# Gated heads: the head's choice of output expert is applied in the turned layout, by masks made with 0/1 products

## The reference, cut to what matters

```python
q, k = heads(x @ w_q), heads(x @ w_k)              # 8 heads of 64
gates = sigmoid(x @ w_gate)                        # 8 experts for each head and token
sel = argmax(gates, axis=-1)
gm = one_hot(sel, 8) * gates                       # one gate value at one of 8 places
values = einsum('bhne,ehdk,bnd->bhnk', gm, value_experts, x)
attn = softmax(where(causal, (q * 64**-0.5) @ k.T, -big))
out = attn @ values                                # z, 64 wide for each head
out = einsum('bhne,ehkd,bhnk->bhnd', gm, output_experts, out)
x = x + out.sum(over heads)
```

## Time and profile before

| what | value |
|---|---|
| median of three runs | 3925.12 us (3923.46 to 3925.54) |
| the profiled execution: its time, its span | 3947.5 us, 3945.8 us |
| busy, share of the span | PE 3584.7 us (91%), PEld 2967.5 (75%), DVE 2856.1 (72%), ACT 2172.8 (55%), POOL 299.6 (8%) |
| mean granted TensorE clock | 0.968 |
| the stage `gated_heads` | from 2759 us to the end |

### The profile page before, as it was taken

How to read it: one execution, slowest core, us unless ns; L and a number is a source line. 1 busy time by engine, 2 the same in 40 slices (tenths; PEclk the granted TensorE clock), 3 DMA queues, 4 the chain that set the end, 5 groups by cost and what they waited for, 6 DMA issues and landing times. The chain is left out here.

```text
span 3945.8 us, 93353 instructions
## 1 busy us (share of the span) xinstructions
PE 3584.7 (91%) x28930; PEld 2967.5 (75%) x28930; DVE 2856.1 (72%) x9189; ACT 2172.8 (55%) x6677; POOL 299.6 (8%) x382
## 2 busy tenths in 40 slices
PE   6999999899999998079877889998899999999998
PEld 5888888688888886069755656665688888888887
DVE  5666666677777777556567878887877787777786
ACT  5777777677777776235444557776433333333333
POOL 0000000000000000521287000000000000000000
PEclk9999999899999999589989999999999999999999
DMA  2000000100000002422211000000200000000000
GB/s 98 0 0 0 0 0 0 38 33 11 11 11 11 11 11 97 143 92 77 73 43 37 0 20 21 21 21 19 92 12 13 8 11 13 8 13 11 11 11 9
DMA packets 56112, 109.74 MB, mean 28 GB/s; under 512 B 8368, under 2 KB 27184, under 8 KB 55728
## 3 DMA queue, kind: packets, MB, share of 16 engines
q1 hardware_dynamic: 46656, 80.72, 6.5%
q0 software_dynamic: 8464, 26.22, 2.0%
q10 hardware_dynamic: 864, 1.19, 0.1%
HBM read 72.46 MB, written 35.65 MB: 27 GB/s over the span
## 5 line engine op out<-in xcount | busy, mean ns | idle before, releaser
L639 ACT ACTIVATE c_pr<-c_sm,c_nmx 128x256 f32<-128x256 f32 x512 | 254.5, 499 | 153.5 <-DVE c_nmx L485 153.5
L127 PE MATMUL f_ps_out<-f_out_rounded,f_zgT 128*128 128x256 f32 x1024 | 310.3, 303 | 0.0
L128 PE MATMUL f_ps_out<-f_out_rest,f_zgT 128*128 128x256 f32 x1024 | 288.5, 282 | 0.0
L129 PE MATMUL f_ps_out<-f_out_rounded,f_zgT 128*128 128x256 f32 x1024 | 286.3, 280 | 0.0
L639 ACT ACTIVATE a_pr<-a_sm,a_nmx 128x128 f32<-128x128 f32 (+1 forms) x512 | 227.1, 444 | 105.9 <-DVE a_nmx L485 105.8
L485 DVE CUSTOM_DVE_ANT_0 a_sm<-a_ps_s,causal 128x128 f32<-128x128 f32 (+1 forms) x512 | 152.6, 354 | 164.3 <-PE a_ps_s L371 164.3
L2170 DVE TENSOR_TENSOR f_gv<-f_ps_v,f_gm_step 128x512 f32<-128x512 f32 x256 | 175.8, 687 | 124.9 <-PE f_ps_v L129 112.7
L2329 ACT CAST f_zgT<-f_ps_g 128x512 fp32r<-128x512 f32 x256 | 151.4, 591 | 204.8 <-PE f_ps_g L2059 204.8
L1770 ACT ACTIVATE c_pr<-c_ps_s,c_nmx 128x256 f32<-128x256 f32 x512 | 214.2, 500 | 87.5 <-DVE c_nmx L1602 87.5
L485 DVE CUSTOM_DVE_ANT_0 c_sm<-c_ps_s,c_mask 128x256 f32<-128x256 f32 x512 | 186.8, 421 | 92.0 <-PE c_ps_s L371 90.2
L2229 DVE TENSOR_TENSOR f_zgT<-f_ps_g,f_zgT 128x512 fp32r<-128x512 f32 x256 | 176.6, 690 | 77.3 <-ACT f_zgT L2329 73.6
(11 more groups left out here) (380 smaller groups left out, 11382.7 us busy)
## 6 DMA issues: line engine op xcount, KB each, us to landing
f_slot_rows<-f_run POOLq DMA_DIRECT2D x1, 9216.0 KB, 34.7
f_rows<-f_slot_rows SPq DMA_DIRECT2D x72, 128.0 KB, 2.0
f_slot_out<-f_y SPq DMA_DIRECT2D x72, 128.0 KB, 1.9
c_ctx_stage<-in_ctxT SPq DMA_DIRECT2D x32, 256.0 KB, 2.8
small<-in_f_w SPq DMA_DIRECT2D x16, 512.0 KB
x_sb<-in_x SPq DMA_DIRECT2D x8, 512.0 KB, 8.1
small<-in_c_w SPq DMA_DIRECT2D x8, 512.0 KB, 3.8
c_mask_stage<-in_mask SPq DMA_DIRECT2D x16, 256.0 KB, 3.0
```

The source lines that it names most:

```text
L127: nc.tensor.matmul(out, sh, mh, start=start, stop=False, **kw)
L128: nc.tensor.matmul(out, sh, ml, start=False, stop=False, **kw)
L129: return nc.tensor.matmul(out, sl, mh, start=False, stop=stop, **kw)
L639: last = nc.scalar.activation(pr[:, r, i, 0:n], sm[:, j, i, 0:n], ACT.Exp, bias=nmx[:, j, i:i + 1], scale=-1.0, accum_out=sums[:, r, i:i + 1])
```

## The change

Mask and gate value are separated. The gate value (`top`) multiplies the softmax's division in `norm`, as a second pointer, so z comes out of `values` already gated once. The choice itself, now exactly 0 or 1 (`one`), is turned once a batch (`turn_one` on PE into `ps_t`, `take_one` on ACT, four copies of 32 partitions to `oneT`). For each step `spread_one` makes, by products with a constant 0/1 matrix `spread` (built by POOL at the stage's start, behind which PE, DVE and ACT wait by the semaphore `made`), the mask of one expert over 128 rows (two heads of 64) and 256 tokens, two experts for each k, in `ps_g`. z is split into rounded part and rest once a step (`take_zT` on ACT, `rest_z` on DVE), and `gate_z` multiplies both parts by the mask from `ps_g`, two DVE instructions of 128 x 512 for each k, to `zgT`. `back`, `take_z`, `turn_zg`, `take_zgT`, `rest_zgT`, `cut_piece` and `keep_piece` are gone. k now counts pairs of experts, not (j, i); `output` keeps its 12 products for each k, and the output experts lie in another order (`f1_out`). The output's lag is 4 (`OUT_LAG`), while `LAST` stays 5. `choose` takes the minimum of 1 + exp(-logit) and the reciprocal of the 16 minima only, where it took the reciprocal of all 128 values.

```diff
+            nc.gpsimd.memset(one[:], 0.0).then_inc(made, 1)
+            nc.gpsimd.memset(sel, 0.0).then_inc(made, 1)
+            pool.wait_ge(made, 2)
+            nc.gpsimd.affine_select(out=sel, in_=sel, compare_op=ALU.not_equal, fill=1.0, base=0,
+                                    pattern=[[-1, E], [-E, 2], [0, 64]], channel_multiplier=1).then_inc(made, 1)
+            for s in range(STEPS):
+                nc.gpsimd.tensor_copy(oneT[:, s, :], one[:].rearrange("p i s n -> p (i s n)")).then_inc(made, 1)
+            pool.wait_ge(made, 3)
+            nc.gpsimd.tensor_copy(spread[:], sel).then_inc(made, 1)
...
+                if s == STEPS - 2 and j == 0:
+                    pe.wait_ge(oneT_ready, b + 1)
...
-            def back(g, s):
-                pe.wait_ge(zT_ready, g + 1)
+            def turn_one(b):
+                pe.wait_ge(pick_s, PICKS * (b + 1))
+                pe.wait_ge(prT_ready, 2 * (STEPS * b + 2))
                 for i in range(ST):
-                    last = nc.tensor.transpose(ps_z[:, S + i * P:S + (i + 1) * P], zT[:, s % 2, i * P:(i + 1) * P], c.ident[:])
-                last.then_inc(backed, 1)
-            def turn_zg(g, s, k, batches):
-                pe.wait_ge(zg_ready, K * g + k + 1)
+                    last = nc.tensor.transpose(ps_t[:, i * P:(i + 1) * P], one[:, i].rearrange("p s n -> p (s n)"), c.ident[:])
+                last.then_inc(one_ps, 1)
+            def spread_one(g, s, k, b, batches):
                 if late(g, 1) or k:
                     pe.wait_ge(zgT_ready, K * g + k)
-                if s == STEPS - LAST % STEPS and k == 0:
+                if s == 0 and k == 0:
+                    pe.wait_ge(oneT_ready, b + 1)
                     pe.wait_ge(gate_exp, batches)
-                for p in range(E // 2):
-                    last = nc.tensor.transpose(ps_g[:, p * P:(p + 1) * P],
-                                               zg[:, k % 2, 2 * p:2 * p + 2, :].rearrange("p e k -> p (e k)"), c.ident[:])
-                last.then_inc(zg_ps, 1)
+                for n in range(2):
+                    last = nc.tensor.matmul(ps_g[:, n * S:(n + 1) * S], spread[:, 2 * k + n].rearrange("p j m -> p (j m)"),
+                                            oneT[:, s, :], start=True, stop=True)
+                last.then_inc(spread_ps, 1)
 
             def output(g, s, k, b):
-                j, i = k // 2, k % 2
                 pe.wait_ge(zgT_ready, K * g + k + 1)
                 if s == 0 and k == 0 and late(g, STEPS):
                     pe.wait_ge(added, b)
-                if not late(b, 1) and i == 0:
-                    pe.wait_ge(pieces.split, HEADS + 2 * s + j + 1)
-                for p in range(E // 2):
-                    last = product3(nc, ps_out[:, i * D:(i + 1) * D], [t[:, k % 2, p, :] for t in zgT],
-                                    [t[:, 2 * s + j, p, :] for t in w_out], s == 0 and k == 0 and p == 0,
-                                    s == STEPS - 1 and j == 1 and p == E // 2 - 1, skip_group_check=True)
+                if not late(b, 1) and k % 2 == 0:
+                    pe.wait_ge(pieces.split, HEADS + 2 * s + k // 2 + 1)
+                for n in range(2):
+                    for i in range(ST):
+                        last = product3(nc, ps_out[:, i * D:(i + 1) * D], [zgT[:, k % 2, r, n, i * P:(i + 1) * P] for r in range(2)],
+                                        [t[:, 2 * s + k // 2, (2 * k + n) % 4, :] for t in w_out],
+                                        s == 0 and k == 0 and n == 0 and i == 0,
+                                        s == STEPS - 1 and k == K - 1 and n == 1, skip_group_check=True)
...
+                if late(b, 1):
+                    dve.wait_ge(top_kept, STEPS * b)
+                done(nc.vector.tensor_reduce(top[:], gate[:], X, ALU.min))
+                done(nc.vector.tensor_tensor(eq[:], gate[:], wide(top), ALU.is_equal))
                 done(nc.vector.tensor_tensor(eq[:], eq[:], rev[:], ALU.mult))
                 done(nc.vector.tensor_reduce(best[:], eq[:], X, ALU.max))
-                done(nc.vector.tensor_tensor(eq[:], eq[:], wide(best), ALU.is_equal))
                 if late(b, 1):
 
-                    dve.wait_ge(piece, STEPS * b)
-                done(nc.vector.tensor_tensor(gm[:], eq[:], gate[:], ALU.mult))
-            def cut_piece(g, s):
+                    dve.wait_ge(v_gated, K * STEPS * b)
+                done(nc.vector.tensor_tensor(gm[:], eq[:], wide(best), ALU.is_equal))
+                done(nc.vector.reciprocal(top[:], top[:]))
+                if late(b, 1):
+                    dve.wait_ge(one_ps, b)
+                for i in range(ST):
+                    done(nc.vector.tensor_copy(one[:, i, :, 0:2 * E], gm[:, i * HEADS:(i + 1) * HEADS, :].rearrange(
+                        "p (s j) e -> p s (j e)", j=2)))
+                done(nc.vector.tensor_tensor(gm[:], gm[:], wide(top), ALU.mult))
...
-                    last = nc.vector.tensor_scalar(pr[:, r, keys(i)], pr[:, r, keys(i)], inv[:, r, i:i + 1], None, ALU.mult)
+                    last = nc.vector.tensor_scalar(pr[:, r, keys(i)], pr[:, r, keys(i)], inv[:, r, i:i + 1],
+                                                   top_step[:, s, j, i:i + 1], ALU.mult, ALU.mult)
...
+            def rest_z(g, s):
+                dve.wait_ge(zT_round, g + 1)
+                nc.vector.tensor_tensor(zT[:, s % 2, 1, :], ps_z[:, 0:S], zT[:, s % 2, 0, :].bitcast(F32),
+                                        ALU.subtract).then_inc(zT_ready, 1)
...
+                dve.wait_ge(spread_ps, K * g + k + 1)
+                dve.wait_ge(zT_ready, g + 1)
                 if late(g, 1) or k >= 2:
 
-                    dve.wait_ge(zg_ps, K * g + k - 1)
-                nc.vector.tensor_tensor(zg[:, k % 2], z[:, i, 64 * j:64 * j + 64].unsqueeze(1).broadcast_to([P, E, 64]),
-                                        gm_late[:, s, i, j, :].unsqueeze(2).broadcast_to([P, E, 64]), ALU.mult).then_inc(zg_ready, 1)
+                    dve.wait_ge(out_ps, K * g + k - 1)
+                for r in range(2):
+                    last = nc.vector.tensor_tensor(zgT[:, k % 2, r], zT[:, s % 2, r, :].bitcast(F32).unsqueeze(1).broadcast_to([P, 2, S]),
+                                                   ps_g[:].rearrange("p (n s) -> p n s", n=2), ALU.mult)
+                last.then_inc(zgT_ready, 1)
...
             def take_zT(g, s):
                 act.wait_ge(z_done, g + 1)
                 if late(g, 2):
-                    act.wait_ge(backed, g - 1)
-                nc.scalar.copy(zT[:, s % 2, :], ps_z[:, 0:S]).then_inc(zT_ready, 1)
-            def take_zgT(g, k):
-                act.wait_ge(zg_ps, K * g + k + 1)
-                if late(g, 1) or k >= 2:
-                    act.wait_ge(out_ps, K * g + k - 1)
-                nc.scalar.copy(zgT[0][:, k % 2].rearrange("p e s -> p (e s)"), ps_g[:]).then_inc(zgT_round, 1)
+                    act.wait_ge(zgT_ready, K * (g - 1))
+                nc.scalar.copy(zT[:, s % 2, 0, :], ps_z[:, 0:S]).then_inc(zT_round, 1)
+            def take_one(b):
+                act.wait_ge(one_ps, b + 1)
+                for s in range(STEPS):
+                    last = nc.scalar.copy(oneT[0:32, s, :], ps_t[32 * s:32 * s + 32, 0:S])
+                last.then_inc(oneT_ready, 1)
...
-        "f1_out": v["L1_ffn_output_experts"].reshape(4, 2, 8, 64, D).transpose(1, 3, 2, 0, 4).reshape(P, 8, 4, D),
+        "f1_out": v["L1_ffn_output_experts"].reshape(8, 4, 2, 64, D).transpose(2, 3, 1, 0, 4).reshape(P, 8, 4, D),
```

More of the change, by code:

```diff
@@ L2088, in slot @@
                         project_v(now[0], s, k, b)
-                    if k == 1 and one:
-                        scores(one[0], one[1], now[0] + 1 if now else one[0] + 1)
+                    if k == 1 and ahead:
+                        scores(ahead[0], ahead[1], now[0] + 1 if now else ahead[0] + 1)
                     if k % 2 and two:
-                        turn(two[0], two[1], k // 2)
-                    if five:
-                        turn_zg(five[0], five[1], k, b + 1 if now else B)
+                        turn(two[0], two[1], k // 2, two[2])
+                    if four:
+                        spread_one(four[0], four[1], k, four[2], b + 1 if now else B)
                         if k:
-                            output(five[0], five[1], k - 1, five[2])
+                            output(four[0], four[1], k - 1, four[2])
                 if s == STEPS - 1 and (not isinstance(b, int) or b + 1 < B):
@@ L2100, in slot @@
                     values(at[0], at[1])
-                if five:
-                    output(five[0], five[1], K - 1, five[2])
+                if four:
+                    output(four[0], four[1], K - 1, four[2])
+                if now and s == STEPS - 1:
+                    turn_one(b)
             turn_x(0)
+            pe.wait_ge(made, MADE)
             run_steps(pe, STEPS, slot, LAST)
@@ L2224, in add_to_x @@
```

(39 more changed lines are left out.)

78 lines of the change are left out of this document (30 added, 48 removed).

## The result

The changed kernel takes 3912.71 us (median of 7 runs, 3904.14 to 3918.92), the kernel before 3923.46 beside it (7 runs, 3920.25 to 3932.72): ratio 0.9969, 95% interval 0.9957 to 0.9980. That is 10.8 us faster, where 46 were predicted.

What follows compares the result with a forecast made beforehand. PE, busy for the whole steady batch of 71.64 us, was taken as the bound. Steady -36.9, ramp +4.2, tail -14.7 and start +1.1 sum to -46.3 us off the median 3925.12: 3879 us, range 3860 to 3906.

Steps and rivals of the forecast that it cites:

- The batch's first slot: `choose` at the batch's head: starts 1.8 us after `gates`, no PE pause, only 0.2 us of cover.
- Rival A: PE pauses more, from dearer DVE products or a late first-slot group: 3890 to 3914 us; chance 0.20.
- start: Stage start: PE waits for POOL's constants and begins later, +1.1 us, bounds 0 and +8.
- step 4: Ramp: DVE-bound step also carries output work with the shorter lag, 14.4 to 18.6 us, +4.2.
- steps 5 to 7: First steady slots after the ramp: their share of the -36.9 us steady gain, -1.9.
- 13 batches of the loop: Steady loop: saving of 2.50 us a batch, -32.5 us of the -36.9 steady sum.
- last batch and tail: Final steady batch plus the slots without projections after step 63: -17.2 us together.
- PE per slot: Steady slot on PE: transposes removed, 8 spreading products added at 0.117 us each, 0.76 us less a slot.
- x: Time each of DVE's two gating products holds DVE: 0.605 us.
- rival C: DVE's two gating products cost 0.9 us each, making the kernel slower: 3948 us; chance 0.05.
- The predicted pause ahead of `output(3)`: PE waits for DVE before a slot's last `output`, 0.09 us a slot.
- Tail: After step 63: four slots instead of five, 1.9 us a k for 2.12, 41.3 us in all, -14.7.

Runs made afterwards that it cites:

- with 16: Changed kernel with 16 idle semaphore increments put ahead of DVE's work in the stage: 3873.18 us, ratio 0.9847 to 0.9877.
- the three runs: Changed kernel with 16, 50 or 117 idle semaphore increments ahead of DVE's work in the stage: 3873.18, 3869.03 and 3877.03 us.
- with 122: Changed kernel with 122 idle semaphore increments ahead of DVE's work in the stage: 3939.96 us, ratio 1.0027 to 1.0056.
- the kernel before with 22: Kernel before the change, with 22 idle semaphore increments ahead of DVE's work in the stage: 3966.43 us, ratio 1.0083 to 1.0114.
- 50: Changed kernel with 50 idle semaphore increments ahead of DVE's work in the stage: 3869.03 us, ratio 0.9846 to 0.9876.
- 117: Changed kernel with 117 idle semaphore increments ahead of DVE's work in the stage: 3877.03 us, ratio 0.9859 to 0.9900.
- the kernel with more cover: Changed kernel, unpadded, `take_one` moved behind the gates' exponential and the copies into `one` to the slot's end: ratio 0.9885 to 0.9918.

## Why the prediction was wrong

The step that failed is "**The batch's first slot** ... No pause, but only 0.2 us of cover". The changed kernel waits 2.05 to 2.33 us there, from the loop's second turn on. The prediction's reasons were nearly right: `choose` was to start 1.8 us after `gates`, and in three pieces it starts 2.02 after (3285.54 less 3283.52), with a wait of 0.2 to 0.4 us for PE. What I left out is that the slot begins with the loop's jump back, which in the changed kernel costs DVE 2.1 us and 0.5 more; `choose` starts 3.81 after `gates` (3298.80 less 3294.99). The mechanism is not in any row of before, since before had no fetch there; its slot was safe by 18 instructions. Rival A had the place, and 3912.71 lies in its 3890 to 3914, but that is luck: the cause that it names is worth 0.4 us a batch, as the run with `take_one` moved shows (the copies hold ACT 0.37 apiece, not 0.28; the prediction had 0.4 a batch as a bound), and the jump is the rest.

Term by term, distances in the traces, in us:

| term | predicted | changed | with 16 |
|---|---|---|---|
| start: POOL's first to PE's first | +1.1 | +0.9 | +0.9 |
| steps 0 to 3 | 0 | -0.5 | -0.5 |
| step 4 | +4.2 | +8.6 | +9.6 |
| steps 5 to 7 | -1.9 | -3.9 | -3.9 |
| 13 batches of the loop | -32.5 | +2.1 | -40.9 |
| last batch and tail | -17.2 | -17.3 | -18.3 |

(The predicted -36.9 and -14.7 are cut at the same places. The changed kernel's terms sum to -10.1, those with 16 to -53.1.)

- PE per slot: 0.76 less was predicted, 0.96 came (17.58 to 16.62). The products of `spread_one` are 0.12 apart as said; `back` was worth about 0.2, not 0.14, and `turn` takes 0.08 less ahead of the new group (0.31 for 0.39 at k = 1), twice a slot.
- `gate_z`: x was right. 681 ns each, and the pair of instructions holds DVE 1.2; rival C is out. The Trainium skill, "VectorE: DVE Perf Modes", section on the TRN2 errata, gives a Vector instruction 62 cycles more when its source is PSUM than from SBUF. The trace does not agree: 681 ns with PSUM as a source, 683 from SBUF alone. `norm` costs 407 ns for 256 elements, as taken from L2117. The predicted pause ahead of `output(3)`, 0.09 a slot, did not appear. The groups of DVE, 3223 to 3295 us:

```profile
L2234 DVE TENSOR_TENSOR f_zgT<-f_zT,f_ps_g 128x512 fp32r<-128x512 f32 x32 | 20.4, 681 | 0.0
...
L2218 DVE TENSOR_SCALAR f_pr<-f_pr,f_inv,f_top_step 128x256 f32<-128x256 f32 x8 | 3.3, 407 | 0.0
```

- Step 4 was sized at 18.6 us and took 23.0, with a wait of PE of 3.0 us in it: `choose` and a rounding of weights share DVE's first microseconds there.
- Start: POOL works from 2736.01 to 2741.20, 5.2 us for 5.4 predicted.
- Tail: four slots; a k takes 1.88 us (1.9 predicted), with one wait a slot:

```profile
3892.17 0.50 PE L2071 MATMUL f_ps_g<-f_oneT,f_spread 128*128 128x256 f32 x2 [1.38 <-DVE f_zgT L2234]
...
3894.05 0.50 PE L2071 MATMUL f_ps_g<-f_oneT,f_spread 128*128 128x256 f32 x2
```

Where the loop lies in three pieces, as before, the change thus takes the kernel to 3869 to 3877 us (the last with 6 us of padding in it), near the forecast of 3879. That nearness is in part luck: the batches gave 8 us more than was summed, and step 4 took 5 more. From the first `gates` to the end the three runs take 43 to 45 us less than the changed kernel; by the medians the place took 36 to 44.

## What to carry to other kernels

An edit moves all code behind it. Where an engine runs a loop of hundreds of instructions, look at the loop's head after each edit: an idle time with "issue" as its releaser there, and packets on the instruction queue in the middle of a loop, mean that the code is fetched anew each time; then a few idle instructions ahead of the loop may be worth more than the edit. Compare two versions only at a place where both fit. And let the batch's critical chain not begin right behind the jump back.

## What the hardware showed that I had not expected

- Instructions for DVE come in packets of 8 KB, and a loop may lie in three such pieces; in four, five packets come a turn (why four pieces are not held, and why five packets come for them, stays open). The jump back then takes DVE's sequencer 2.8 to 3.1 us instead of 0.29 (3.4 to 4.1 with 122 and in the kernel before with 22, where the second fetch is met in the same stop); 1.8 to 2.1 of the 2.8 to 3.1 are seen as idle time of DVE, since it still had work.
- The Trainium skill, "Runtime: NRT & Kernel Launch", section on instruction fetch, has the mechanism: a taken branch whose target lies outside the held pages stalls for a fetch. It gives two pages of 256 instructions each. These runs do not agree: a body of 279 would then be dear at 22 neighbouring places of 256, but paddings of 0 and 122 are dear and 16, 50 and 117 between them are not. The measurement decides.
- A wait of PE of 2.1 to 2.3 us in the changed kernel goes with 3.4 us, once 6.8, at a granted clock of 0.50, which cost about 1.5 us beyond the wait (PE busy 69.84 against 68.30 a batch). The length of the wait alone does not decide it: in the kernel before with 22, three of twelve batches keep clock 1.00 with waits of 1.9 to 2.3 us, and of two waits of 1.8 us in the kernel with more cover one had the lower clock.
